# A transformer tower on one core: new slots for every stage, and the gate multiply and the last add moved from VectorE to GpSimd

## What is computed

```python
h = combined @ W                                    # position, nesting and segment rows of tables
x = layernorm(h)
q, k, v = split(x @ qkv_w.T + qkv_b)                # 8 heads of 16
h = h + softmax(q @ k.T / 4) @ v @ out_w.T + out_b
y = layernorm(h)
g = softmax(y @ gate_w.T) - sigmoid(y @ thr_w.T) / 4
w = max(g, 0) / sum(max(g, 0))                      # sum 0 counts as 1
hidden = relu(y @ fc1_w[e].T)                       # 4 experts
h = h + sum_e w[e] * (hidden @ lora_A[e] @ lora_B[e] @ fc2_w[e].T)
```

## Time and profile before

| | us |
| --- | --- |
| median of 3 runs | 1270.05 (1269.89 to 1274.09) |
| the profiled execution, its own time | 1273.26 |
| its span in the trace | 1271.4 |
| TensorE busy | 1154.3 (91%) |
| VectorE busy | 952.3 (75%) |
| ScalarE busy | 821.4 (65%) |
| GpSimd busy | 592.9 (47%) |

### The profile page before, as it was taken

How to read it: one execution, slowest core, us unless ns; L and a number is a source line. 1 busy time by engine, 2 the same in 40 slices (tenths; PEclk the granted TensorE clock), 3 DMA queues, 4 the chain that set the end, 5 groups by cost and what they waited for, 6 DMA issues and landing times.

```text
span 1271.4 us, 20444 instructions
## 1 busy us (share of the span) xinstructions
PE 1154.3 (91%) x6392; PEld 435.5 (34%) x6392; DVE 952.3 (75%) x2402; ACT 821.4 (65%) x1602; POOL 592.9 (47%) x588
## 2 busy tenths in 40 slices
PE   3479899999999999999999999999999999999984
PEld 1123333333333333333333333333333333333322
DVE  6388777787778877877877788788877877877522
ACT  1127677776776776666777776667677667776751
...
DMA packets 88376, 123.97 MB, mean 98 GB/s; under 512 B 17469, under 2 KB 69054, under 8 KB 82054
## 3 DMA queue, kind: packets, MB, share of 16 engines
...
## 4 chain that ended last, share of the span: by engine, by line
PE 32%; DVE 27%; DMA 16%; ACT 8%; issue 5%; ACTq 1%; POOL 1%; SPq 0%; POOLq 0%; DVEq 0%
DVE negmax L877 13%; DMA den_dram<-ctx_sb 11%; PE pv L633 9%; PE mix L643 5%; PE mix L695 5%; PE sc L622 4%; DMA den<-den_dram 4%; DVE bn L867 4%; ACT probs L485 3%; PE mix L665 3%; PE mix L678 2%; PE mix L660 2%; ACT ctx_sb L535 2%; DVE h L901 2%; ACT qk L496 1%
## 5 line engine op out<-in xcount | busy, mean ns | idle before, releaser
L877 DVE TENSOR_REDUCE negmax<-mix 128x1 f32<-128x512 f32 x1024 | 666.5, 681 | 153.3 <-PE mix L643 151.9
L485 ACT ACTIVATE probs<-sc 128x512 f32<-128x512 f32 x1024 | 593.1, 600 | 220.1 <-PE sc L622 192.0
L622 PE MATMUL sc<-qstk,kstk 120*128 120x512 bf16 x1024 | 383.8, 382 | 1.2 <-DMA qstk<-mT 0.5
L643 PE MATMUL mix<-kstk,qstk 96*128 96x512 bf16 x1024 | 356.2, 391 | 18.3 <-ACT wT L555 5.5
L633 PE MATMUL pv<-probs,vals 128*32 128x512 f32 x2048 | 273.5, 606 | 0.0
L438 POOL TENSOR_TENSOR ctxh<-ctx_sb,rdenb 128x512 f32<-128x512 f32 x64 | 81.3, 1271 | 391.5 <-DMA rdenb<-rden_dram 390.9
L643 PEld LDWEIGHTS mix<-kstk,qstk 96*128 96x128 bf16 x1024 | 100.2, 99 | 346.5 <-DVE negmax L877 166.7
L622 PEld LDWEIGHTS sc<-qstk,kstk 120*128 120x128 bf16 x1024 | 100.2, 98 | 124.8 <-ACT probs L485 54.6
L695 PE MATMUL mix<-xn2T,fc1T_sb 128*128 128x512 f32 x256 | 136.6, 616 | 1.0 <-DVE negmax L877 1.0
L405 POOL TENSOR_TENSOR pieces<-qk,pieces 128x512 bf16<-128x512 f32 x64 | 73.9, 1154 | 71.2 <-ACT pieces L500 71.2
L560 ACT ACTIVATE hid<-mix 128x512 f32<-128x512 f32 x128 | 77.6, 606 | 28.7 <-PE mix L695 28.7
...
## 6 DMA issues: line engine op xcount, KB each, us to landing
stack_dram<-pieces SPq DMA_DIRECT2D x192, 128.0 KB
...
```

The costliest lines, as they stand in the source:

```text
L485: act.activation(probs[:, c % 8, i % 2], sc[:, i % RING], ACT.Exp).then_inc(s_exp, 1)
L622: pe.matmul(sc[:, i % RING, :], kstk[0:KROWS, u, h, j * P:(j + 1) * P], qstk[0:KROWS, u, h, :], start=True, stop=True).then_inc(s_score, 1)
L643: pe.matmul(max_bank(m), qstk[0:STK, u, h, j * P:(j + 1) * P], kstk[0:STK, u, h, :], start=True, stop=True).then_inc(s_mxmm, 1)
L877: dve.tensor_reduce(negmax[:, m // NT, m % NT:m % NT + 1], max_bank(m), AX.X, ALU.max, negate=True).then_inc(s_max, 1)
```

## The change

- Every stage has a new slot, and the max tiles of a sequence begin in slot 8 instead of 10. `hot`, `embed`, `add_pos` and layer norm 1 work four sequences ahead instead of three (the loop begins one step earlier), `v` three instead of two, and the statistics are done in two halves.
- `weigh`: ScalarE copies the bank of `low` to SBUF (`copy_low`), GpSimd multiplies it in place. `finish`: ScalarE copies the bank of `out` (`copy_out`), GpSimd adds `h2` in place. The semaphores `s_lo32` and `s_out32` free the banks.
- ScalarE issues no DMA in the loop any more: `store_den`, `store_weights` and `load_max` go to SP's list.
- The copy of the gate logits is gone; the gate chain reads the PSUM bank.
- `h2` has two buffers instead of four, with two new waits in `add_attention`; `hb_sb` has five instead of four.

```diff
-MSTART = 10
+MSTART = 8
 RING, MIX = 3, 4
 U = 4
+HB, H2 = 5, 2
 PE_ORDER = [("max", 0), ("scores", 0), ("product", 0), ("scores", 1), ("max", 1), ("values", 0)]
 PRODUCTS = [
-    ("project", -2), ("embed", 3), ("low", -3), ("v", 2), ("out", -3), ("xn2T", -2), ("gates", -2), ("fc1_0", -2),
-    ("turn_gates", -2), ("xnT", 3), ("fc1_1", -2), ("q", 3), ("mT", 1), ("k", 3), ("fc1_2", -2), ("fc1_3", -2),
+    ("project", -2), ("xnT", 3), ("q", 3), ("low", -3), ("k", 3), ("xn2T", -2), ("out", -3), ("gates", -2),
+    ("turn_gates", -2), ("v", 3), ("fc1_0", -2), ("embed", 4), ("mT", 1), ("fc1_1", -2), ("fc1_2", -2), ("fc1_3", -2),
 ]
 ACT_WORK = [
-    (3, 1, "v", 2, 0), (4, 0, "ctx", -1, 1), (4, 1, "den_out", -1, 1), (5, 1, "xn2T", -2, 0), (6, 1, "gates", -2, 0),
-    (7, 1, "relu", -2, 0), (8, 2, "gate_exp", -2, 0), (9, 1, "xnT", 3, 0), (10, 1, "relu", -2, 1),
-    (11, 1, "qk", 3, 0), (12, 0, "ctx", 0, 0), (12, 1, "mT", 1, 0), (12, 2, "max_in", 1, 0), (13, 0, "wT", -2, 0),
-    (13, 0, "weights_out", -2, 0), (13, 1, "qk", 3, 1), (13, 2, "den_out", 0, 0), (14, 1, "relu", -2, 2),
+    (1, 1, "xnT", 3, 0), (2, 1, "qk", 3, 0), (3, 1, "low", -3, 0), (4, 0, "ctx", -1, 1), (4, 2, "qk", 3, 1), (5, 2, "xn2T", -2, 0),
+    (6, 1, "out", -3, 0), (7, 1, "gates", -2, 0), (9, 0, "gate_exp", -2, 0), (9, 1, "v", 3, 0), (10, 1, "relu", -2, 0),
+    (12, 0, "ctx", 0, 0), (12, 1, "mT", 1, 0), (12, 2, "wT", -2, 0), (13, 1, "relu", -2, 1), (14, 1, "relu", -2, 2),
     (15, 1, "relu", -2, 3),
 ]
 DVE_WORK = [
-    (0, 0, "hot", 3, 0), (0, 1, "add_attention", -2, 0), (0, 2, "stats2", -2, 0), (1, 0, "moments2", -2, 0),
-    (1, 1, "add_pos", 3, 0), (2, 0, "stats1", 3, 0), (2, 1, "weigh", -3, 0), (2, 2, "moments1", 3, 0),
-    (4, 1, "finish", -3, 0), (7, 0, "invert_den", -1, 0), (8, 1, "gate", -2, 0), (9, 0, "gate", -2, 1),
-    (10, 0, "gate", -2, 2), (11, 0, "gate", -2, 3),
+    (0, 1, "add_attention", -2, 0), (1, 0, "stats2", -2, 0), (1, 1, "stats2", -2, 1), (2, 0, "moments2", -2, 0),
+    (7, 1, "invert_den", -1, 0), (8, 1, "gate", -2, 0),
+    (9, 1, "gate", -2, 1), (9, 2, "hot", 4, 0), (10, 0, "gate", -2, 2), (10, 0, "gate", -2, 3),
+    (11, 1, "add_pos", 4, 0), (12, 0, "stats1", 4, 0), (12, 1, "stats1", 4, 1), (13, 0, "moments1", 4, 0),
 ]
 POOL_WORK = [
-    ("add_bias", 2, 0), ("rstd2", -2, 0), ("norm2", -2, 0), ("rstd1", 3, 0), ("norm", 3, 0), ("normalise", -1, 0), ("second", 3, 0),
-    ("residual", 3, 0), ("third", 3, 0), ("second", 3, 1), ("residual", 3, 1), ("third", 3, 1),
+    ("add_bias", 3, 0), ("rstd2", -2, 0), ("norm2", -2, 0), ("weigh", -3, 0), ("second", 3, 0),
+    ("residual", 3, 0), ("third", 3, 0),
+    ("second", 3, 1), ("finish", -3, 0), ("residual", 3, 1), ("third", 3, 1), ("normalise", -1, 0), ("rstd1", 4, 0), ("norm", 4, 0),
 ]
 SP_WORK = [
-    ("ids", 4, 0), ("out", -3, 0), ("den_in", -1, 0), ("rden_out", -1, 0), ("rden_in", -1, 0),
-    ("piece", 3, (0, 0)), ("weights_in", -2, 0), ("piece", 3, (0, 1)), ("piece", 3, (0, 2)), ("piece", 3, (1, 0)),
-    ("piece", 3, (1, 1)), ("piece", 3, (1, 2)), ("stack", 3, 0), ("stack", 3, 1),
+    ("ids", 4, 0), ("piece", 3, (0, 0)), ("den_out", -1, 1), ("piece", 3, (0, 1)), ("piece", 3, (0, 2)),
+    ("den_in", -1, 0), ("piece", 3, (1, 0)), ("piece", 3, (1, 1)), ("out", -3, 0), ("piece", 3, (1, 2)),
+    ("rden_out", -1, 0), ("rden_in", -1, 0), ("stack", 3, 0), ("stack", 3, 1), ("den_out", 0, 0), ("max_in", 1, 0),
+    ("weights_out", -2, 0), ("weights_in", -2, 0),
 ]
...
-            for t in range(-3, NSEQ + 3):
+            for t in range(-4, NSEQ + 3):
...
+            def store_den(b, g, u):
+                upto(sp, s_ctx, b, 2, g + 1)
+                upto(sp, s_denin, b - 1, 16)
+                row = (HC, 0)[g]
+                sp.dma_start(den_dram[4 * g:4 * g + 4], ctx_sb[row:P:Q, u % 2, g, :]).then_inc(s_denout, 16)
+
+            def store_weights(b):
+                upto(sp, s_wT, b)
+                upto(sp, s_win, b - 1, 16)
+                for r in range(WREP):
+                    sp.dma_start(w_dram[:, r].rearrange("e (j n) -> j e n", n=P), wT[:]).then_inc(s_wout, 16)
+
+            def load_max(b, u):
+                upto(sp, s_mT, b)
+                sp.dma_start(qstk[STK:KROWS, u, :, :],
+                             mT[:].unsqueeze(1).broadcast_to([3 * NH, NH, S])).then_inc(s_mrow, 16)
+
...
-                upto(pool, s_h2, b - U)
-                pool.tensor_tensor(hb_sb[:, u], h_sb[:], obias[:].unsqueeze(1).broadcast_to([P, NT, P]),
+                upto(pool, s_h2, b - HB)
+                pool.tensor_tensor(hb_sb[:, b % HB], h_sb[:], obias[:].unsqueeze(1).broadcast_to([P, NT, P]),
...
+            def weigh(b):
+                upto(pool, s_lo32, b)
+                upto(pool, s_win, b, 16)
+                pool.tensor_tensor(low[:], low[:], wrow[:], ALU.mult).then_inc(s_low, 1)
+
+            def finish(b):
+                upto(pool, s_out32, b)
+                upto(pool, s_h2, b)
+                pool.tensor_tensor(out_sb[:], out_sb[:], h2[:, b % H2], ALU.add).then_inc(s_out, 1)
...
+            def copy_low(b):
+                upto(act, s_lomm, b)
+                upto(act, s_outmm, b - 1)
+                act.copy(low[:], aux("low", 1)).then_inc(s_lo32, 1)
+
+            def copy_out(b):
+                upto(act, s_outmm, b)
+                upto(act, s_store, b - 1, 16)
+                act.copy(out_sb[:], aux("out")).then_inc(s_out32, 1)
...
-                "turn_gates": (turn_gates, (s_logit, 1, 1)),
+                "turn_gates": (turn_gates, (s_gate, 13, 3)),
...
-                "low": (low_rank, (s_low, 1, 1)),
+                "low": (low_rank, (s_lo32, 1, 1)),
...
-                "out": (experts_out, (s_out, 1, 1)),
+                "out": (experts_out, (s_out32, 1, 1)),
...
-            def stats(b, src, bn, s_src, s_bn):
+            def stats(b, src, bn, s_src, s_bn, half):
                 upto(dve, s_src, b)
-                for j in range(NT):
+                for j in (2 * half, 2 * half + 1):
...
-                dve.tensor_tensor(h2[:, u], aux("project"), hb_sb[:, u], ALU.add).then_inc(s_h2, 1)
+                upto(dve, s_hc2, b - H2)
+                upto(dve, s_out, b - H2)
+                dve.tensor_tensor(h2[:, b % H2], aux("project"), hb_sb[:, b % HB], ALU.add).then_inc(s_h2, 1)
...
-                dve.tensor_copy(logit[:], aux("turn_gates", 1)[:, 0:P].rearrange("p (j q) -> p j q", q=Q)[:, :, 0:NE + 1]
-                                ).then_inc(s_logit, 1)
-                upto(dve, s_logit, b)
+                logit = aux("turn_gates", 1)[:, 0:P].rearrange("p (j q) -> p j q", q=Q)
                 dve.tensor_reduce(lmax[:], logit[:, :, 0:NE], AX.X, ALU.max).then_inc(s_gate, 1)
+
+                dve.tensor_scalar(lsub[:, :, NE:NE + 1], logit[:, :, NE:NE + 1], -1.0, 87.0,
+                                  ALU.mult, ALU.min).then_inc(s_gate, 1)
                 upto(dve, s_gate, b, 13, 1)
                 dve.tensor_tensor(lsub[:, :, 0:NE], logit[:, :, 0:NE], lmax[:].unsqueeze(2).broadcast_to([P, NT, NE]),
```

More of the change, by code:

```diff
@@ L193, in tower @@
         gat = sb("gat", [P, P])
-        logit = sb("logit", [P, NT, 5])
         lmax = sb("lmax", [P, NT])
@@ L363, in _ @@
                 "weights_in": lambda b, u, _: load_weights(b),
+                "max_in": lambda b, u, _: load_max(b, u),
+                "den_out": lambda b, u, g: store_den(b, g, u),
+                "weights_out": lambda b, u, _: store_weights(b),
                 "out": lambda b, u, _: store_out(b),
@@ L372, in _ @@
             nc.disable_value_cache = True
-            load_ids(0)
             steps(sp, step)
@@ L455, in _ @@
                 "norm": lambda b, u, _: norm(b),
+                "weigh": lambda b, u, _: weigh(b),
+                "finish": lambda b, u, _: finish(b),
                 "normalise": lambda b, u, _: normalise(b, u),
@@ L512, in copy_mT @@
                 act.copy(mT[:], aux("mT", 1)[0:3 * NH]).then_inc(s_mT, 1)
-            def store_den(b, g, u):
-                upto(act, s_ctx, b, 2, g + 1)
-                upto(act, s_denin, b - 1, 16)
-                row = (HC, 0)[g]
-                act.dma_start(den_dram[4 * g:4 * g + 4], ctx_sb[row:P:Q, u % 2, g, :]).then_inc(s_denout, 16)
-            def store_weights(b):
-                upto(act, s_wT, b)
-                upto(act, s_win, b - 1, 16)
-                for r in range(WREP):
-                    act.dma_start(w_dram[:, r].rearrange("e (j n) -> j e n", n=P), wT[:]).then_inc(s_wout, 16)
-            def load_max(b, u):
-                upto(act, s_mT, b)
-                act.dma_start(qstk[STK:KROWS, u, :, :],
-                             mT[:].unsqueeze(1).broadcast_to([3 * NH, NH, S])).then_inc(s_mrow, 16)
             def copy_ctx(b, g, u):
@@ L566, in _ @@
                 "relu": lambda b, u, e: relu(b, e),
+                "low": lambda b, u, _: copy_low(b),
+                "out": lambda b, u, _: copy_out(b),
                 "wT": lambda b, u, _: copy_wT(b),
```

(16 more changed lines are left out.)

13 lines of the change are left out of this document (6 added, 7 removed).

## The result

The changed kernel takes **1346.8 us** (median of 4 runs, 1340.75 to 1352.65) against 1272.1 us (4 runs) for the kernel before on the same chip: ratio 1.059, 95% interval 1.056 to 1.061. The forecast of 1242 us was on the wrong side; the mechanism is that of the rival "max_in comes later still", and its size was larger than the 1287 us given there. The prediction's own sign of being wrong came true as well: the first score matmul of a step waits more than 2 us (2.8 in the mean of 25 steps). The profiled span is 1343.8 us.

A forecast was written before the change was run, and what follows sets the result against it. With TensorE 91% busy, its stalls were the target; afterwards the DMA chain to max_in would set the step. 36.41 - 35.3 = 1.1 us for 27 steps (-30), then -2, +1, +1.8: 1244, against the median 1242 us; range 1218 to 1274.

The forecast's parts named there:

- max_in comes later still: Rival on SP's queue: max_in lands over 36.6 us into a step; at 37.0 a step loses 0.6, 1287 us; chance 0.15.
- The prediction's own sign of being wrong: At a step's first score matmul: it never waits and the step is 34.6 us, or it waits over 2 us.
- The step becomes 35.3 us, set by the DMA chain.: Loop step through GpSimd, SP and max_in: 35.3 us against 36.41 before, TensorE waiting some 0.7 us at its start.
- the DMA part: From the first stack load at 23.1 us to max_in's landing at 35.3, with 1.77 MB taking 9.7 us.
- The chain ahead of the stack loads: GpSimd's and SP's operations from a step's start: third ends at 18.7 us, stack loads begin at 23.1.
- So I cost them at nothing: GpSimd's two added operations fall beside VectorE's reduces from PSUM: no cost, at most 2 x 1.27 us.
- 34.0 us for a step with no stall: TensorE's loop step without stalls: 34.0 us, from 36.41 and stalls of 2.6 in the mean of 25 steps.
- the stalls of slots 2, 3 and 13 gone: TensorE's stalls of 0.25, 0.69 and 0.37 us in these slots were to disappear.
- the denominators' wait: VectorE's wait for den's DMA at the reciprocal, 1.44 us in one step, falls below 0.5 a step.
- For TensorE and VectorE alone: Step set by these two engines only: about 34.6 us, with 0.3 to 0.8 us of stall in place of 2.4.
- The point from which the change loses: The change is slower once max_in lands more than 36.6 us after the step's start.
- the later bound: Later end for max_in's landing, 35.9 us into the step, if rdenb goes ahead of the stacks; the earlier is 34.3.

The follow-up runs named there:

- the two best kernels: The changed kernel with stack loads last in SP's list, plus either weigh and finish on VectorE (1202.9 us) or finish behind normalise on GpSimd (1203.0 us).

## Why the prediction was wrong

**"The step becomes 35.3 us, set by the DMA chain."** The chain was the right one, with the releaser and the place that the prediction named; its length was 39.1. What failed above all is the term for the DMA part, 12.2 us from the first stack load to max_in's landing; it measured 14.8. Two smaller things were missing.

- *The DMA part* (12.2, measured 14.8 in the mean of 25 steps, 13.7 to 15.9; 2.6 of the 3.8 us). It was costed as 1.5 us until bytes flow, 9.7 for 1.77 MB at 182 GB/s, and 1.0 for the part of rdenb that comes first. But in the kernel before, the stack loads alone (1.57 MB) took 11.6 us from the first issue to the last landing. In the changed kernel, where rdenb's 0.5 MB are issued 0.7 and 1.7 us ahead of them, they take 14.0, and the next step starts 0.8 us after the last one has landed. With max_in ahead of the stacks they are issued at least 6.7 us behind rdenb and take 11.6 again. The last piece, from issue to landing (count, KB, us), in the changed kernel and with max_in ahead (8.4 before):

```profile
kstk<-stack_dram SPq DMA_DIRECT2D x32, 128.0 KB, 10.9
...
kstk<-stack_dram SPq DMA_DIRECT2D x32, 128.0 KB, 8.6
```

  That rdenb is what lengthens them is argued from this comparison; with the stacks last, where max_in and the gate weights go just ahead, they take 13.7. The prediction also calls the stretch from 606 full, where the earlier trace rows have a DMA share of 0.48. And the rate in the loop is not steady. It is above 182 GB/s at first and far below it at the end, where the last stack pieces and max_in land:

```profile
686.00:694.00 8.00, 8.00 (x43) 2.78 (x42) 6.58 (x20) 6.47 (x14) 3.96 (x4) 1.00 1.00 217
694.00:698.46 4.46, 2.39 (x14) 0.45 (x12) 2.05 (x4) 1.60 (x4) 3.11 (x4) 1.00 0.41 79
```

- *The chain ahead of the stack loads* (23.1, measured 24.25 in the mean). The walk was right for a step that starts at full clock: 23.4, with third of k at 18.9 for the forecast 18.7. It left out that the wait at a step's start can be followed by a half clock, as in 11 of 25 steps. In those the moments come 1.0 us later, and ScalarE, late by the same slots, hands over `low` after GpSimd is free (0.70 us of idle time at 669.34); the stack loads begin at 25.3 and the step takes 40.3 us instead of 38.1. So the loop lengthens itself, but the steps without that still take 38.1.
- *The clock* is in no term of the sum. Its 0.8 us a step are the same loss as the later start of the stack loads, seen on TensorE; they are not to be added.

**"So I cost them at nothing"**, of GpSimd's two operations beside VectorE. The prediction put the conflict at `hot`, `wsafe` and `wts`, which indeed became free, and placed the two added operations beside reduces. But `finish` stands ahead of `residual` and `third` for k, and pushes these onto the casts in slot 8. What was missed is not the price of an overlap but whom the delayed operations meet. 1.24 us of stall at v, against 0.3 to 0.8 forecast for v and embed together; 32 us in the run with the stacks last.

**What was right.** 34.0 us for a step with no stall (34.2 in the two best kernels; its own 36.41 less 2.6 would be 33.8, a slip that changes nothing); the stalls of slots 2, 3 and 13 gone; the denominators' wait below 0.5 a step (14.4 us in 32); `wts` short again. For TensorE and VectorE alone 34.6 was forecast; with the stacks last it is 35.3 with the casts held up and 34.2 without. The point from which the change loses, 36.6 us, was right too (36.7 us a step went with 1276.0 us). That the later bound lay 0.7 us below it was the weak argument: both bounds shared the same GpSimd walk and the same rate, so they did not bound those two.

**What stays open.** How much of the 2.6 us of the DMA part is rdenb's, since no run moved it alone; why max_in on ScalarE's queue was not served earlier; and why a half clock followed some waits and not others as long.
